# A network kernel of 2,460 lines: seven loops over bands written as loops on the engines instead of laid out flat

## The reference, cut to what matters

```python
x = x + _L0_conv_ref(_gn(x), ...)   # two 3x3 convolutions in hyperbolic space, with a batch norm and a ReLU after each
x = x + _L1_conv_ref(_gn(x), ...)   # a Laplace operator: DFT of the even rows and columns, residues at 4 x 4 poles, evaluation
x = x + _L2_conv_ref(_gn(x), ...)   # windows of 8 x 8: layer norm, four Kolmogorov-Arnold layers, their sum
x = x + _L3_conv_ref(_gn(x))        # soft local binary pattern of the 8 neighbours: sigmoid(10 * (neighbour - centre))
```

## Time and profile before

| | |
|---|---|
| median of 3 runs | 10979.16 us (10977.14 to 10985.86) |
| the profiled execution | 10979.16 us, its span 10977.4 us |
| instructions recorded | 357,918 |
| busy share of the span | PE 81%, PEld 41%, DVE 84%, ACT 77%, POOL 0% |
| the window layer | 4465 to 10210 us, ACT 5587.6 us busy, DVE 5366.1 us, PE 4791.4 us |
| the two convolutions | 280 to 1400 and 1440 to 2560 us, PE 1001.3 and 1007.6 us busy |

### The profile page before, as it was taken

How to read it: one execution, slowest core, us unless ns; L and a number is a source line. 1 busy time by engine, 2 the same in 40 slices (tenths; PEclk the granted TensorE clock), 3 DMA queues, 4 the chain that set the end, 5 groups by cost and what they waited for, 6 DMA issues and landing times. The chain is left out here.

```text
span 10977.4 us, 357918 instructions
## 1 busy us (share of the span) xinstructions
PE 8837.5 (81%) x158370; PEld 4448.7 (41%) x158370; DVE 9180.9 (84%) x10651; ACT 8401.7 (77%) x5579; POOL 0.2 (0%) x4
## 2 busy tenths in 40 slices
PE   0889879996665798688888888888888888888688
PEld 0344334333443686333333333333333333333355
DVE  6777756666777698799999999999999999998788
ACT  0555545554662543799999999999999999999698
POOL 0000000000000000000000000000000000000000
PEclk9999989998887999799999999999999999999899
DMA  7999879995673586555555555555555555555576
GB/s 286 249 258 256 237 217 264 263 263 211 273 276 108 169 279 234 94 107 109 112 109 106 107 108 108 112 108 106 109 107 108 111 110 108 106 106 98 154 216 194
DMA packets 1196580, 1826.06 MB, mean 166 GB/s; under 512 B 135201, under 2 KB 956449, under 8 KB 1124769
## 3 DMA queue, kind: packets, MB, share of 16 engines
q1 hardware_dynamic: 1195040, 1803.15, 65.0%
HBM read 717.88 MB, written 411.04 MB: 103 GB/s over the span
## 5 line engine op out<-in xcount | busy, mean ns | idle before, releaser
L1968 DVE SCALAR_TENSOR_TENSOR grown_ex<-ratio,ex 128x2048 f32<-128x2048 f32 x1024 | 2332.4, 2287 | 83.9 <-issue 33.3
L1846 ACT ACTIVATE ex<-ex 128x2048 f32<-128x2048 f32 x1024 | 1925.5, 1898 | 4.1
L2101 PE MATMUL out<-ex,kan_basis 32*32 32x512 f32 x32768 | 1427.5, 639 | 539.4 <-DVE z L1950 361.7
L2101 PE MATMUL out<-grown_ex,kan_basis 32*32 32x512 f32 x32768 | 1551.9, 629 | 55.3 <-DVE grown_ex L1968 42.8
L556 PE MATMUL conv<-uc,w 128*32 128x512 f32 x12288 | 1451.6, 598 | 17.2 <-DMA uc<-u 16.8
L1842 ACT ACTIVATE ex<-kin,offset 128x2048 f32<-128x2048 f32 x512 | 1013.3, 1991 | 48.2 <-PE out L2101 42.1
L463 ACT ACTIVATE v<-conv,cb 128x512 f32<-128x512 f32 x512 | 350.8, 685 | 907.2 <-PE conv L556 406.8
L2101 PEld LDWEIGHTS out<-grown_ex,kan_basis 32*32 32x32 f32 x32768 | 543.5, 106 | 657.6 <-issue 563.8
L2101 PEld LDWEIGHTS out<-ex,kan_basis 32*32 32x32 f32 x32768 | 395.1, 106 | 1001.2 <-issue 927.9
L556 PEld LDWEIGHTS conv<-uc,w 128*32 128x32 f32 x12288 | 495.7, 109 | 725.6 <-issue 674.5
L2240 DVE TENSOR_TENSOR d<-xt 128x2313 f32<-128x2313 f32 (+2 forms) x256 | 621.8, 2495 | 94.6 <-PE acc L2294 94.3
(11 more groups left out here) (282 smaller groups left out, 16020.4 us busy)
## 6 DMA issues: line engine op xcount, KB each, us to landing
uc<-u SPq DMA_DIRECT2D x2048, 129.0 KB, 3.5
xt<-in_x SPq DMA_DIRECT2D x128, 1024.0 KB, 7.4
t<-v SPq DMA_DIRECT2D x128, 1024.0 KB, 9.8
back_k<-ku SPq DMA_DIRECT2D x1024, 128.0 KB
xt<-in_x SPq DMA_DIRECT2D x32, 2048.0 KB, 7.6
xt<-t SPq DMA_DIRECT2D x64, 1024.0 KB, 6.8
tt<-t SPq DMA_DIRECT2D x64, 1024.0 KB, 12.0
x<-x SPq DMA_DIRECT2D x64, 1024.0 KB, 4.9
```

Source lines behind the costliest of these rows:

```text
L1846: a.activation(ex[:, j], ex[:, j], ACT.Exp, scale=-1.0).then_inc(exps, 1)
L1968: v.scalar_tensor_tensor(grown_ex[:, j % 2], ratio[:], LARGEST, ex[:, j], ALU.min, ALU.mult).then_inc(grown, 1)
L2101: last = m.matmul(out[rows(i), g, :], k["kan_basis"][rows(g), kind - 1, n, :], base[rows(g), cols(i)], start=(n == 0), stop=(n == BASES - ...
```

## The change

Seven Python loops become `Fori` loops. The loop's body then stands once in the stream of each engine that runs it; the loop variable is a register, stepped at the end of the body and compared for the jump back. Each count of a wait and each address that depends on the loop variable is computed on the engine, in registers. The step functions are written for both kinds (they ask `isinstance(t, int)`). The first and last rounds, the order of the steps, the tiles and the transfers are as before. TensorE and SyncE of the pattern layer stay flat.

```diff
 def pipeline(eng, count, stages):
...
-    for t in range(deep + 1, count):
+    with eng.Fori(deep + 1, count) as t:
         for lag, step in stages:
             step(t - lag)
...
 def pipeline_by_two(eng, count, stages):
...
-    for t in range(first // 2, count // 2):
+    with eng.Fori(first // 2, count // 2) as t:
         for parity in range(2):
             round_(t * 2 + parity, parity)
...
 # conv_layer, rounds
-            for pair in range(2, BANDS // 2 - 1):
+            with eng.Fori(2, BANDS // 2 - 1) as pair:
                 for parity in range(2):
                     round_(pair * 2 + parity, parity)
...
 # residual_layer, two_bands
-            for pair in range(1, BANDS // 2 - 1):
+            with eng.Fori(1, BANDS // 2 - 1) as pair:
                 band(pair * 2, 0)
                 band(pair * 2 + 1, 1)
...
 # window_layer, rounds
-            for r in range((STAGES + 2) // 2, BANDS):
+            with eng.Fori((STAGES + 2) // 2, BANDS) as r:
                 for h in range(HALVES):
                     round_(Round(r * 2 + h, h))
...
 # pattern_layer, VectorE
-            for pair in range(1, BANDS // 2 - 1):
+            with dve.Fori(1, BANDS // 2 - 1) as pair:
                 band(pair * 2, 0)
                 band(pair * 2 + 1, 1)
...
 # pattern_layer, ScalarE
-            for r in range(2, BANDS):
+            with act.Fori(2, BANDS) as r:
                 band(r)
```

## The result

The changed kernel took 11224.9 us in the median (11213.2 to 11228.1, 4 runs) beside 10978.2 us for the kernel before: a ratio of 1.0219 (95% interval 1.0205 to 1.0232), 247 us slower. The forecast was 11,270 us, slower, within 11,050 to 11,620.

What follows compares the result with a forecast made beforehand. VectorE and ScalarE were taken as full in the window layer, over half the span. Window layer 145 us plus other stages 145 us, on 10979.16 us, gave 11,270 us; range 11,050 to 11,620 with rivals, 11,130 to 11,430 without.

Steps and rivals of the forecast that it cites:

- VectorE full, its wait list the proof: Window layer: VectorE waits for others only 41.7 us in 5380 us, so time its queue loses beyond slack lengthens the span.
- The place: Window layer: VectorE's jump falls drained between the measurement's copy and the next product, every second tile, about 3 us exposed.
- The price of the jump: VectorE, window layer: 2.8 us fetch (from bounds of 2.4 to 3.1) plus 0.3 us jump, 3.1 us a pair exposed.
- The rule of the Trainium skill: A taken branch outside the two blocks held waits for a fetch; VectorE's body, about 400 instructions, exceeds a 256-instruction block.
- Register arithmetic: Window layer, VectorE: 38 values a pair computed behind drains at 0.06 us each, 2.3 us a pair (0.8 to 3.0).
- The slack of 1.4 us a pair: Window layer: VectorE's waits for others, 1.4 us in each pair of tiles, subtracted from the cost of jump and arithmetic.
- The bound of 28 us on what a straight stream costs VectorE: VectorE, whole kernel: about 70 blocks of 256 instructions at 0.4 us a gap, the largest gain allowed.
- Late hand-over: Window layer: TensorE, ScalarE and SyncE hand work on late, 1.0 us a pair (between 0 and 3).
- rival 2: Several engines' stalls add up in the window layer's ring, 9 to 10 us a pair; about 11,550 us, chance 0.18.
- The other stages: Outside the window layer: convolutions 52, residual layer 28, evaluation 42, residues 15, input statistics and pattern layer 8; together 145 us.
- The straddling of blocks: Window layer: ScalarE's and SyncE's bodies, about 220 and 170 instructions, are likely to straddle two blocks.
- The term of 3.1 us for VectorE in the evaluation: Evaluation of residues: VectorE ends each of 6 passes drained, so its jump costs 3.1 us a pass.

Runs made afterwards that it cites:

- w_dve_two: Changed kernel with VectorE's window loop holding two pairs of tiles a pass, the last pair laid out flat: 11129.1 us.
- w_dve_head0: Changed kernel with VectorE's window loop placed at the first slot of an instruction block, no hint: 11079.8 us.
- w_dvehint_peflat: Changed kernel with TensorE's window walk flat and a prefetch hint in VectorE's window loop; ScalarE and SyncE looped: 11076.9 us.
- w_dvepe_flat: Changed kernel with VectorE's and TensorE's window walks laid out flat; ScalarE and SyncE looped: 11009.0 us.
- w_dve_flat: Changed kernel with only VectorE's window walk laid out flat; TensorE, ScalarE and SyncE looped: 11097.6 us.
- w_dve_hint: Changed kernel with a prefetch hint for the jump back in VectorE's window loop; all four engines looped: 11074.2 us.
- w_flat: Changed kernel with the window layer's middle laid out flat on all four engines, the other loops kept: 11004.4 us.
- w_act_two: Changed kernel with VectorE and TensorE flat in the window layer and ScalarE's loop holding two pairs a pass: 11003.9 us.

## Why the prediction was right, step by step

*VectorE full, its wait list the proof.* Right. VectorE's 28 jumps hold 142 us of gaps in the changed kernel and 7 with the hint, and the time fell by 151; ScalarE, busier by the table, could stall 2.6 us for nothing.

*The place.* Right: one idle stretch "by issue" between the measurement's copy and the next product at every second tile, 0.2 us at the others. VectorE's body has 352 recorded instructions where I had counted about 400.

*The price of the jump.* Too small. The forecast had 2.8 + 0.3 = 3.1 us. The wait list from 4850 to 10000 us, with 27 jumps, gives (192.2 - 67.5) / 27 = 4.6 us a jump, the times 151 / 28 = 5.4 (the forecast counted 29; the last pass does not jump). The term that was mis-sized is the 2.8 us of the fetch. It held on ScalarE, whose gap was 2.4 to 2.8 us. On VectorE even a single packet took 4.1 to 4.5 us (w_dve_two): it starts 2.3 us after the comparison, where ScalarE's starts 0.9 us after, and VectorE goes on some 2 us later. In the changed kernel two packets are read one after the other (in the pass shown at 7056.7 and 7059.3 us) ahead of the first instruction behind the jump, and the gap is 4.9 us in the median. So the second read is a small part of the error, and why VectorE's fetch takes so much longer than ScalarE's stays open. The upper bound in that step was no bound.

*The rule of the Trainium skill.* The Trainium skill's page "Runtime: NRT & Kernel Launch", section "Instruction fetch mechanics", was right in what decides: a taken branch to a block that is no longer held stands until it is read, and flat code is better for it. These traces agree: 4.9 us on VectorE with a read, 0.27 without. Its size of a block, 256 instructions, is not what VectorE's queue moved, which was packets of 128. Two blocks of 256 would hold the 352 instructions of w_dve_head0; in the blocks that were measured these fill three and were not read again, so more than two of those are held.

*Register arithmetic.* The price stood: 2.3 us a pair forecast, and 0.3 for the jump itself; 68 / 29 = 2.3 us a pass measured for both together, with no fetch (w_dvehint_peflat against w_dvepe_flat). The slack of 1.4 us a pair, which I took off, was not spent: VectorE's waits for others rose by 28 us there and did not shrink. That these waits lie in other places than the drained steps is my reading, not shown. The bound of 28 us on what a straight stream costs VectorE took blocks of 256; its packets hold 128, so there are twice as many. In the window layer the gaps that the loop took away sum to 15.6 us of 5150 (the eleven rows of w_dvepe_flat).

*Late hand-over.* Forecast at 1.0 us a pair with three engines in it. It was TensorE's alone: 89 us by itself (w_dve_flat against w_dvepe_flat), 3.2 us a pair, the length of its comparison. But it does not add to VectorE's arithmetic. From 11009 us one costs 68, the other 89, and both together 65 (w_dve_hint, 11074). Beside VectorE's hinted loop it makes no difference whether TensorE is looped or flat (11074 and 11077). VectorE's wait for TensorE's product fell from 87.2 us (w_dve_flat) to 40.1 (w_dve_hint), so while VectorE is late by its arithmetic TensorE's stall falls in part into time that is lost already. On top of both, VectorE's fetch costs 151. Added up the three would be 308 us, and the changed kernel is 216 us over w_dvepe_flat, so rival 2, stalls in sequence, fails in its full form. VectorE's fetch beside a flat TensorE was not run.

*The other stages.* Forecast at +145 us, measured at about zero in sum. The convolutions (52), the residual layer (28) and the pattern layer (5) lost nothing: the jumps of VectorE, ScalarE and SyncE took 0.2 to 0.3 us in the median. That the register work there lay ahead of waits would explain the rest and is not shown. Evaluation and residues lost 8 and 12 us where 42 and 15 stood. The straddling of blocks that I feared for bodies under 256 instructions showed in no jump: VectorE's body of 255 in the evaluation went on after 0.32 us, and ScalarE's and SyncE's in the window layer after 0.24 and 0.28. The term of 3.1 us for VectorE in the evaluation has nothing behind it.

So the total came out near by luck, by two errors of opposite sign: 145 us for the window layer where it was 217, and 145 for the rest where the table has 2 (by the times w_flat leaves 28 us over the kernel before, of which its profile has some 17 in the window layer itself).

## What to carry to other kernels

Count an engine's instructions in the body of a loop before writing it as one. A body that the engine still holds when it jumps back costs 0.2 to 0.3 us a pass for the jump. Here no body up to 255 instructions on VectorE, ScalarE or SyncE stalled, and one of 352 on VectorE stalled or not by where it was placed; a longer one on ScalarE (458) paid 2.4 to 2.8 us a jump, VectorE 4.1 to 6.6, TensorE (about 6,500) 3.6. A hint or the placement of the loop's head took it all away on VectorE's 352. Then look at what stands in the queue at the jump: behind a drain on VectorE all of it showed, behind ScalarE's 2 us operation and with its slack none. And register arithmetic cost 2.3 us a pass, jump included, on VectorE, the engine without slack whose steps stand behind drains, and nothing on ScalarE and SyncE in the window layer.

## What the runs showed of the hardware that was not expected

- The two instruction queues read in different portions: 16.4 KB packets (256 instructions) for TensorE, 8.2 KB (128) for the others. Flattening TensorE's walk moved only the first queue (1110 to 1055 packets), changing VectorE's only the second.
- Where a loop's head lies in its block decides some 5 us a pass (145 us in 28 jumps): 352 instructions of VectorE from slot 0 read nothing again (71 packets in the run), from where the change had put them five packets a pass.
- A stalled jump is recorded differently: on TensorE as a comparison of 3.6 us, on VectorE and ScalarE as a comparison of 45 to 63 ns and a gap behind it (5.8 and 2.6 us in the passes shown).
- On VectorE the stall was nearly twice as long as on ScalarE, also where both read a single packet at the jump (4.1 to 4.5 us in w_dve_two, 2.4 to 2.8 in w_act_two). The number of blocks read is not the reason; what is stays open.
- With the prefetch hint VectorE's loop read no packet at all, while TensorE's, hinted, still read one at its jumps and its comparison took 0.7 us in the median.
